# A routed expert loop on TensorE: rows transposed three tiles ahead, down products two tiles back, expert numbers held in three-digit packs

## What is computed

```python
x = x + attention(layernorm(x))
z = layernorm(x)
scores = sigmoid(z @ gate_w.T + lb_bias)          # 8 experts
topw, topi = top_k(scores, 2); topw /= topw.sum(-1) + 1e-8
for e in range(8):
    m = (topi == e); wmean = (topw * m).sum() / max(m.sum(), 1)
    y = (silu(z @ gate[e].T) * (z @ up[e].T)) @ down[e].T     # hidden width 128
    out += where(m.any(-1), y * wmean, 0)
out += (silu(z @ sgate.T) * (z @ sup.T)) @ sdown.T            # shared expert, hidden width 256
x = x + out
```

## Time and profile before

| | us |
|---|---|
| median of 3 runs (548.74 to 550.45) | 550.24 |
| the profiled execution's own time | 550.23 |
| its span, first to last instruction | 548.4 |
| PE busy in the span | 515.2 (94%) |
| DVE busy | 392.0 (71%) |
| ACT busy | 338.1 (62%) |
| POOL busy | 228.7 (42%) |

### The profile page before, as it was taken

One profiled execution on the slowest core, in us unless ns is written; L12 is line 12 of the kernel. 1 busy time (PEld: TensorE's weight loads), 2 busy tenths in 40 slices (PEclk: granted clock), 3 DMA queues, 4 the chain that ended last, 5 costly groups with the idle time before them and its releaser, 6 DMA issues.

```text
span 548.4 us, 16371 instructions
## 1 busy us (share of the span) xinstructions
PE 515.2 (94%) x5529; PEld 415.2 (76%) x5529; DVE 392.0 (71%) x1194; ACT 338.1 (62%) x776; POOL 228.7 (42%) x419
## 2 busy tenths in 40 slices
PE   6799999999999999999999678899999999999997
PEld 4567777777777777777778457788888887779996
DVE  6566788888889888878977657746666665552865
ACT  4667787887878778787777423316666666662111
POOL 5100111354245334525533536704555555554751
PEclk9999999999999999999999978979999999999999
DMA  7160101312331321221021134866455554426994
GB/s 215 62 212 5 42 4 42 91 48 88 100 99 37 102 90 39 96 102 72 26 82 62 64 138 143 266 199 213 152 159 156 151 156 131 143 90 211 398 399 159
DMA packets 42559, 69.16 MB, mean 126 GB/s; under 512 B 9708, under 2 KB 28655, under 8 KB 42480
## 3 DMA queue, kind: packets, MB, share of 16 engines
q1 hardware_dynamic: 33984, 43.46, 24.9%
q0 software_dynamic: 6480, 17.31, 8.9%
q10 hardware_dynamic: 2016, 7.34, 4.0%
HBM read 36.43 MB, written 32.06 MB: 125 GB/s over the span
## 4 chain that ended last, share of the span: by engine, by line
PE 81%; ACT 7%; DVE 5%; issue 4%; another core or an unknown queue 1%; POOL 1%; DMA 0%; SPq 0%; POOLq 0%; DVEq 0%; ACTq 0%
PE ps L571 41%; PE ps L630 8%; PE ps L660 6%; PE ps L823 5%; PE ps L914 4%; PE ps L669 3%; PE ps L625 3%; PE ps L582 3%; PE ps L646 2%; PE ps L675 2%; ACT probs L1018 2%; ACT pvs L1025 1%; PE ps L931 1%; ACT vm L991 1%
## 5 line engine op out<-in xcount | busy, mean ns | idle before, releaser
L513 POOL DMA_INDIRECT z_slots<-z,slot x64 | 64.3, 1004 | 123.7 <-PE ps L675 82.7
L571 PE MATMUL ps<-wF,wA 128*128 x639 | 105.2, 303 | 1.0 <-issue 0.4
L556 POOL DMA_INDIRECT y_rows<-vm,dest x71 | 69.6, 980 | 70.6 <-issue 41.2
L571 PEld LDWEIGHTS ps<-wF,wA 128*128 128x128 f32 x639 | 84.9, 188 | 13.9 <-issue 6.4
L1227 DVE TRANSPOSE_TENSOR_REDUCE rmax<-ps 128x32 f32<-128x1024 f32 x64 | 79.6, 1244 | 15.7 <-PE ps L630 14.0
L1018 ACT ACTIVATE probs<-ps 128x1024 f32<-128x1024 f32 x64 | 65.6, 1026 | 31.4 <-PE ps L646 30.7
L630 PE MATMUL ps<-bd,kT 64*128 64x256 f32 x512 | 66.4, 379 | 0.0
L571 PE MATMUL ps<-yT,wA 128*128 128x256 f32 x384 | 61.2, 297 | 1.5 <-DVE yT L1200 1.5
L630 PEld LDWEIGHTS ps<-bd,kT 64*128 64x128 f32 x512 | 49.9, 191 | 5.1
L571 PEld LDWEIGHTS ps<-yT,wA 128*128 128x128 f32 x384 | 49.4, 189 | 4.6 <-issue 1.9
L1125 ACT ACTIVATE vt<-ps 128x256 f32<-128x256 f32 x32 | 12.2, 384 | 58.5 <-PE ps L571 54.7
(11 more groups left out here) (202 smaller groups left out, 1106.6 us busy)
## 6 DMA issues: line engine op xcount, KB each, us to landing
z<-z_slots SPq DMA_DIRECT2D x71, 136.0 KB
zT_scratch<-zT SPq DMA_DIRECT2D x16, 512.0 KB
bd<-y_rows SPq DMA_DIRECT2D x8, 512.0 KB, 10.4
out<-xs SPq DMA_DIRECT2D x16, 256.0 KB, 7.7
wraw_of<-wffn SPq DMA_DIRECT2D x10, 384.0 KB, 4.0
xs<-x SPq DMA_DIRECT2D x7, 512.0 KB, 4.2
wA<-zT_scratch ACTq DMA_DIRECT2D x7, 512.0 KB, 6.4
z<-y_rows SPq DMA_DIRECT2D x4, 512.0 KB, 10.8
```

Source lines behind the costliest of these rows:

```text
L513: eng.indirect_dma_start(z_slots, bass.IndirectOffsetOnAxis(ap=slot[:, c, j, t:t + 1], axis=0), z[:, c, t, :], None, bounds_check=E * REGI ...
L556: eng.indirect_dma_start(y_rows, bass.IndirectOffsetOnAxis(ap=dest[:, m:m + 1], axis=0), yo[:, m, :], None, bounds_check=K * T - 1, oob_is ...
L571: mm = eng.matmul(out, lhsT(a), rhs(b), start=start and n == 0, stop=stop and n == 2, skip_group_check=skip)
```

## The change

Four things are changed, all in or around the tile loop.

1. PE's order in turn `t` becomes `tile_gate_up(t+1)`, `rows_T(t+3)`, `tile_down(t-2)`, `hidden_T(t)`. ACT's becomes `silu(t+1)`, `rows_hi(t+3)`, `scaled(t-2)`, `hidden_hi(t)`. DVE's becomes `hidden(t+1)`, `rows_lo(t+3)`, `hidden_lo(t)`, `destinations(t+1)`. Three waits on PE that the new order makes needless are left out.
2. The expert numbers are packed three to an integer (24 integers). `find_expert` masks the digit where it stands and does not shift; the scale of the digit goes into the multiplication that makes an address. Each tile has a register of its own, so `expert_of` with its copies is gone. The mask stands between the second and the third product of the first gate-and-up group.
3. `weights` takes its address from one flat dimension.
4. POOL waits for `s_y1` alone ahead of a scatter, and the scatter's bound lies in a register that is set once.

```diff
+PACK = 3
 def expert_packs(T):
-    return -(-expert_tiles(T) // 8)
+    return -(-expert_tiles(T) // PACK)
...
+                y_limit = eng.alloc_register("y_limit")
+                eng.reg_mov(y_limit, K * T - 1)
                 def rows_out(q8, m8):
                     t, q, m = later(q8, m8, 0)
-                    wait_apart(eng, s_y1, t + 1)
-                    wait_apart(eng, s_ds, t + 1)
+                    eng.wait_ge(s_y1, t + 1)
                     eng.indirect_dma_start(y_rows, bass.IndirectOffsetOnAxis(ap=dest[:, m:m + 1], axis=0),
-                                           yo[:, m, :], None, bounds_check=K * T - 1, oob_is_err=False
+                                           yo[:, m, :], None, bounds_check=y_limit, oob_is_err=False
...
-                def product(out, lhsT, rhs, start, stop, skip=False):
+                def product(out, lhsT, rhs, start, stop, skip=False, ahead=None):
                     for n, (a, b) in enumerate(((0, 0), (0, 1), (1, 0))):
+                        if n == 2 and ahead:
+                            ahead()
...
                     eng.load(pack_regs, tile_packs[0:1, :])
                     for r in pack_regs:
-                        packs.append(eng.snap(r, min_val=0, max_val=8 ** 8 - 1))
-                expert_regs = [eng.alloc_register(f"expert_{m}") for m in range(4)]
+                        packs.append(eng.snap(r, donate=True, min_val=0, max_val=E ** PACK - 1))
+                experts = {}
                 def find_expert(t):
-                    eng.reg_mov(expert_regs[t % 4], (packs[t // 8] >> (3 * (t % 8))) & (E - 1))
-                def expert_of(t):
-                    return eng.snap(expert_regs[t % 4], min_val=0, max_val=E - 1)
+                    unit = E ** (t % PACK)
+                    r = eng.alloc_register(f"expert_{t}")
+                    eng.reg_mov(r, packs[t // PACK] & ((E - 1) * unit))
+                    experts[t] = eng.snap(r, donate=True, min_val=0, max_val=(E - 1) * unit) * (6 * P // unit)
...
-                def weights(e, a, c0, c1):
-                    return wF[a][:, bass.ds(e, 1), c0:c1].rearrange("p o c -> p (o c)")
+                def weights(at, a, c0, c1):
+                    return wF[a][:, :, :].rearrange("p e c -> p (e c)")[:, bass.ds(at + c0, c1 - c0)]
                 def rows_T(t, q, m):
                     eng.wait_ge(s_zin[m], 16 * (q + 1))
-                    after(eng, s_zl, t - 1)
...
                 def tile_gate_up(t, q, m):
-                    e = expert_of(t)
+                    e = experts[t]
                     eng.wait_ge(s_zl, t + 1)
-                    after(eng, s_h1, t - 1)
...
+                                     ahead=(lambda: find_expert(t + 1)) if k == 0 and t + 1 < NTS else None)
...
                 def hidden_T(t, q, m):
                     eng.wait_ge(s_h1, t + 1)
-                    after(eng, s_hTl, t - 1)
...
                 def tile(q, m):
-                    if 8 * q + m + 2 < NTS:
-                        rows_T(*later(q, m, 2))
                     if 8 * q + m + 1 < NTS:
                         tile_gate_up(*later(q, m, 1))
+                    if 8 * q + m + 3 < NTS:
+                        rows_T(*later(q, m, 3))
+                    if 8 * q + m > 1:
+                        tile_down(*later(q, m, -2))
                     hidden_T(*later(q, m, 0))
-                    if 8 * q + m:
-                        tile_down(*later(q, m, -1))
-                    if 8 * q + m + 2 < NTS:
-                        find_expert(8 * q + m + 2)
```

More of the change, by code:

```diff
@@ L56, in constants @@
     for name, n in (("token", T // P), ("before", P), ("region", E), ("expert", E), ("lower", E * E),
-                    ("upto", E * E), ("tile_rows", T // P), ("tile", expert_tiles(T)), ("choice", K), ("quad", HPT // 2), ("index", 1), ("octal", 8 * expert_packs(T))):
+                    ("upto", E * E), ("tile_rows", T // P), ("tile", expert_tiles(T)), ("choice", K), ("quad", HPT // 2), ("index", 1), ("octal", PACK * expert_packs(T))):
         at[name] = (c, n)
@@ L143, in layer @@
         NPK = expert_packs(T)
-        tile_digits, tile_packs = sb("tile_digits", [P, 8 * NPK]), sb("tile_packs", [P, NPK], I32)
+        tile_digits, tile_packs = sb("tile_digits", [P, PACK * NPK]), sb("tile_packs", [P, NPK], I32)
         tile_sums = sb("tile_sums", [P, NPK])
@@ L929, in hidden_T @@
                         eng.wait_ge(s_tw, 1)
-                    after(eng, s_hTl, t - 1)
                     eng.transpose(ps[:, 6 + m % 2, 0:P], h1[:, m % 2, 1, :], identf[:, :]).then_inc(s_hT, 1)
                 def tile_down(t, q, m):
-                    e = expert_of(t)
+                    e = experts.pop(t)
                     eng.wait_ge(s_hTl, t + 1)
@@ L957, in _ @@
                 find_expert(0)
-                find_expert(1)
                 eng.wait_ge(s_hf, NS * GA)
                 tile_gate_up(0, 0, 0)
+                rows_T(2, 0, 2)
                 down(9)
                 sweep_tiles(eng, tile)
-                eng.wait_ge(s_h1, NTS)
+                tile_down(*later(0, NTS - 2, 0))
                 gate_up(NS * GA)
@@ L1180, in tile @@
                 def tile(q, m):
-                    if 8 * q + m + 2 < NTS:
-                        rows_hi(*later(q, m, 2))
                     if 8 * q + m + 1 < NTS:
                         silu(*later(q, m, 1))
+                    if 8 * q + m + 3 < NTS:
+                        rows_hi(*later(q, m, 3))
+                    if 8 * q + m > 1:
+                        scaled(*later(q, m, -2))
                     hidden_hi(*later(q, m, 0))
-                    if 8 * q + m:
-                        scaled(*later(q, m, -1))
                 silu(0, 0, 0)
+                rows_hi(2, 0, 2)
                 eng.wait_ge(s_tw, 1)
                 sweep_tiles(eng, tile)
+                scaled(*later(0, NTS - 2, 0))
                 scaled(*later(0, NTS - 1, 0))
@@ L1475, in tile_places @@
                     chain(eng.tensor_tensor(tile_digits[:, :], tile_digits[:, :], const("octal"), ALU.mult))
-                    chain(eng.tensor_reduce(tile_sums[:, :], tile_digits[:, :].rearrange("p (n j) -> p n j", j=8), AX.X, ALU.add))
+                    chain(eng.tensor_reduce(tile_sums[:, :], tile_digits[:, :].rearrange("p (n j) -> p n j", j=PACK), AX.X, ALU.add))
                     chain(eng.tensor_copy(tile_packs[:, :], tile_sums[:, :]))
@@ L1581, in tile @@
                 def tile(q, m):
-                    if 8 * q + m + 2 < NTS:
-                        rows_lo(*later(q, m, 2))
                     if 8 * q + m + 1 < NTS:
                         hidden(*later(q, m, 1))
+                    if 8 * q + m + 3 < NTS:
+                        rows_lo(*later(q, m, 3))
                     hidden_lo(*later(q, m, 0))
-                    destinations(*later(q, m, 0))
+                    if 8 * q + m + 1 < NTS:
+                        destinations(*later(q, m, 1))
                 rows_lo(0, 0, 0)
@@ L1591, in _ @@
                 hidden(0, 0, 0)
+                rows_lo(2, 0, 2)
+                destinations(0, 0, 0)
                 sweep_tiles(eng, tile)
@@ L1654 @@
         "index": p[:, None],
-        "octal": 8 ** (np.arange(8 * expert_packs(T)) % 8),
+        "octal": E ** (np.arange(PACK * expert_packs(T)) % PACK),
     }
```

2 lines of the change are left out of this document (1 added, 1 removed).

## The result

The changed kernel takes **558.38 us** (median of 4 runs, 557.06 to 559.83) against 550.27 for the kernel before: a ratio of 1.0176, 95% interval 1.0142 to 1.021. It is slower. The forecast was 531 us, range 526 to 540.

The account below looks back on a forecast made before the run. PE was taken as the bound, slowed by register instructions in its queue. Saving 70 x (1.70 - 1.42) = 19.6 us less 0.5 for loading the packs, 19.1 from 550.23, gave 531 us, range 526 to 540.

Parts of the forecast that it names:

- What bounds the kernel now: Tile loop: PE sets the pace; its queue of 14.8 register instructions makes a tile 1.70 us where the array needs 1.40.
- 0.72 and 0.22 at the joins: Loop's first turn, queue ahead: six gate-and-up products took 0.72 us and two row transposes 0.22, read as the floor.
- POOL: Scatters in the tile loop: 1.28 us a tile, below 1.42, none on the path; the shorter form taken at 0.
- The cover that I named for it: Behind the loop: PE's gapless shared-expert products hide the last scatter; without them the shorter form is worth 0.3 us once.
- The order at nothing: Tile loop: transposes three tiles ahead and down products two back lengthen the hand-offs, so the new order costs 0.
- Loading the packs: PE's stop to load 24 registers instead of nine: 0.5 us more taken, bounds 0 and 2.7 us.
- The end: Start, end and what follows the loop: unchanged but for a few tenths of a us.
- Pauses spread (0.09): Rival, chance 0.09: the pauses of 459 to 485 fill the faster loop, about 10 in 100 us, giving 539 to 541.
- Several engines standing and no releaser: Sign for the spread pauses, 459 to 485: PE busy only 24.59 of 26 us; nearly all the 2.7 us lost there.
- PE has only 0.19 us without work: Sign against the spread pauses: over the 88 us from 371 to 459 PE is almost never without work.
- The slower case (0.04): Rival, chance 0.04: SP's row loads land too late for the transposes, 1.97 us a tile, 16 us over, 566 us.

Follow-up runs that it names:

- plain_gpsimd: The changed kernel with a plain store from GpSimd's queue in place of the indirect scatter: 528.04 us, ratio 0.962.
- direct_store: The changed kernel without indirect scatters, SyncE storing each tile's rows as one plain block: 527.93 us, ratio 0.9593 to the kernel before.
- order_alone: The changed kernel with its order, removed waits and GpSimd part, but the old packs and registers on PE: ratio 1.0158 to the kernel before.
- queue_alone: The kernel before with its old order on all engines and only the leaner PE queue, three waits gone: ratio 1.015.
- spaced512: The changed kernel with a fill of a spare 128x512 tile on GpSimd behind each scatter: span ends at 547.7 us, not faster than the kernel before.
- rest_loop: The kernel before with the leaner scatter and a spare 128x512 fill behind each scatter of the tile loop: ratio 0.9992.
- spaced384: The changed kernel with a fill of a spare 128x384 tile on GpSimd behind each scatter: mean distance 1.69 us, not faster than the kernel before.
- rest_early: The kernel before with a spare 128x512 fill behind each of 16 input-row scatters ahead of the tile loop: ratio 0.9993.
- pad4: The changed kernel with four unread register moves a tile ahead of PE's row transposes: ratio 1.0114 to the kernel before.
- pad6: The changed kernel with six unread register moves a tile ahead of PE's row transposes: ratio 1.0128 to the kernel before.

## Why the prediction was wrong

**What bounds the kernel now** named PE's queue. As to PE this was right. With 9 register instructions a tile for 14.85 it runs at 1.39 to 1.42 us as soon as nothing is held (plain_gpsimd, direct_store), and 0.72 and 0.22 at the joins were no chance of one turn.

**The step that failed** is the *POOL* term taken at 0: "1.28 a tile, below 1.42", and so "none of it is on the path". The cover that I named for it, PE's work behind the loop, was there (busy 51.83 of 52.40 us). What failed is that scatters as close as that cost PE nothing inside the loop. I took GpSimd's 1.28 us, a scatter with its gap, for its limit, and compared it with the period. That row was the fault itself: at 1.28 us apart the increments of PE and the instructions of SyncE are held by up to 2 us, and no run with indirect scatters has a mean distance below 1.68. The kernel before ran at 1.75, just above. So there was, as far as these runs show, a second bound right under the first, and the 0.32 us a tile that PE could give had at most 0.07 us of room. Past that the loop didn't stop at the bound but fell behind it: a held increment stops PE through silu, hidden product and low rows; when it comes, two or three tiles are scaled at once and their scatters follow each other at 1.28 us, which holds the next. That is the cycle of three tiles, 1.82 us each. I read this feedback from the timeline; no run takes it apart link by link. From the first to the last hidden transpose it is 127.3 us, where the forecast's terms give 70 x 1.42 + 2.7 = 102.1. These 25 us are nearly all of 558 - 531 = 27; 1.4 more are the stretch at half clock behind the loop.

**The order at nothing** stays unproved as a step of its own, but order_alone, queue_alone and direct_store agree with it: the hand-offs had room for everything but held increments.

**Loading the packs**, 0.5 us taken: 2.245 - 1.642 = 0.60 measured. **The end** was PE's, as I had it. But the path through the last scatter is only about 2 us shorter: with 9 us gained by PE in the loop (spaced512) it became the bound, and a faster loop gives its whole gain only if the last scatter comes earlier too.

**Pauses spread (0.09)** had the right object and too small a price. "Several engines standing and no releaser" were held increments: the scatter of tile 49, counted from 0, starts late (2.1 us behind its rows' scaling for 0.77 in the kernel before), the next two come 1.3 us apart, and the holds begin; rest_loop has none. I priced them at 10 in 100 us. They were 2.7 in 26 us because the kernel before had its close scatters, 10 of 70, only from there on; in the changed kernel they are 40 of 70 (distances under 1.5 us). "PE has only 0.19 us without work" from 371 to 459 was no evidence against it, since it was true of scatters 1.7 us apart. **The slower case (0.04)** had the right sign and a wrong mechanism: in the waits of the changed kernel from 371 to 499 us PE never waits for a load of rows.

## What to carry to other kernels

A wait that a view puts down to "remote" or to nothing, with several engines standing, is a price to be understood before an engine is made faster, not a constant to be kept. An engine's shortest distance between two operations isn't its sustained rate: look at what the others do while it runs at that distance. Where indirect scatters are frequent, compare the new period with the period at which they run now, and test by moving them together without touching anything else.

## What the runs showed of the hardware

- Indirect scatters of 128 rows from GpSimd that follow each other at less than about 1.6 us hold semaphore increments of TensorE by up to 2.8 us (3.6 ahead of the loop) and stretch SyncE's instructions (29 ns to 701). With 1.68 us from scatter to scatter 2 of 146 increments of TensorE were held (spaced512) or none of 109 (rest_loop), with plain stores 0 of 274. The limit isn't sharp: single distances of 1.56 us held nothing (kernel before), 1.57 again and again held 149 of 221 (spaced384), and ahead of the loop a hold of 1.2 us remained at 1.67 to 1.79 us (rest_early).
- ScalarE's and VectorE's increments aren't held: in the tile loops of all 20 traces none comes more than 13 ns behind its operation. SyncE isn't wholly free at 1.68 us: in spaced512 4 of its 125 register moves in the loop are stretched, up to 506 ns; with plain stores none is over 38 ns. Which resource it is stays open; nothing here shows it.
- The scatter's 0.98 us on GpSimd doesn't show this, since it is the same in the fastest and in the slowest kernel. The Trainium skill ("Perfetto Trace Analysis", DMA Instruction — SWDGE (GPSIMD)) says that such a slice ends when the descriptors are made and not when the data has moved; the trace agrees, since the last scatter of spaced512 has landed only 2.07 us after its start.
- The scatter of tile 49 (counted from 0, so the 50th of the loop, which the expectations call the 49th) starts 1.12 or 2.10 us behind its scaled rows in 16 of the 18 kernels with indirect scatters, 0.85 or 1.33 us more than the least there. It isn't a matter of the indirect form: in plain_gpsimd the plain store of tile 49 does the same (1.62 us for 0.29). Why isn't known.
- Register moves whose result isn't read are missing from the built program (pad4 and pad6: 9 register instructions a tile, as without them).
